# Transformer layer on eight cores: latent weights through the f32 queue, head 0's projections among the latent jobs, value jobs in other steps

## The chip, the cores and the metric

The kernel runs on all eight cores of one Trainium2 chip. The time is device microseconds (us) of the slowest core for one execution. Each core has a tensor engine (PE), a vector engine (DVE), a scalar engine (ACT), GpSimd (POOL) and SyncE (SP); the last two mainly issue DMAs here. A core keeps data in SBUF, and matmuls write to PSUM, which has eight banks of 128 x 512 f32.

## The reference

One pre-norm layer on x of 4 x 2048 x 2048. Attention with a compressed latent for keys and values (16 heads of 128, latent width 512), then a feed-forward part with fp8 weights:

```python
lat = rmsnorm(x @ wkv_a_w.T, norm_w)          # x is layer-normalised before
kv = lat @ wkv_b_w.T                          # keys and values of all heads
q = (x @ wq_w.T + wq_b)                       # the upper 64 of 128 per head rotated
attn = softmax(where(causal, q k^T * scale))  # k rotated in the same way
x = x + (attn @ v) @ out_w.T + out_b
y = layernorm(x)
x = x + (silu(y@gate * gs) * (y@up * us)) @ down * ds   # inner width 6144
```

## The kernel before

Two cores share a batch row. A core owns eight of the sixteen 128-row tiles of the sequence (their queries, outputs and feed-forward part) and computes the latent, keys and values of all sixteen for itself. Nothing passes between cores. Every engine runs a program written out by hand (`sync_prog`, `gpsimd_prog`, `vector_prog`, `scalar_prog`, `tensor_prog`), and they wait for each other on counting semaphores; an engine runs its own list strictly in order. So the place of a job in each of five lists sets the order.

The front. For each of 16 tiles of x (buffers X, four in turn, f32, 1 MB each, loaded by SP): DVE takes statistics (L478), ACT the square root (`sqrt_var`, L681), DVE normalises to bf16 (XH, four buffers, L488), PE transposes in two halves (`transposes`, L781; banks 6 and 7), ACT copies to XQT (tiles 0 to 7, the core's own) or XOT (8 to 15) (`transposed`, L693). Four tiles are a block (tb); for each block PE computes four latent jobs `lat(tb, dl)` of 16 matmuls with 512 columns (L800; block 0 in two halves of 256), one for each 128 of the latent's width, in banks 0 to 3. ACT makes of each its square (LSQ, L699) and a scaled copy (LATU, L702) in `lat_out`. `sumsq` (L811), `rms` on ACT (L707), `diagonal` on DVE (L498) and `broadcast` on PE (L819, bank 5) give the rms factor, and DVE multiplies it in (`latent`, L506) to LATT. The latent weights WKVA are four DMAs from POOL's queue that read f32 and write bf16. In ACT's list `sqrt_var(n + 1)` stands ahead of `lat_out` of tile n. A matmul with M2s and C2Q (L938) makes a small table for the rotation; DVE waits for it after it has normalised tile 5.

Jobs outside the latent have names: Q (h, half; 16 matmuls, L835, copied by DVE L515), K (h, quarter; 4 matmuls, L844, copied by ACT L714), V (group of four heads, tile; 4 matmuls, L854, copied by DVE L528), N, X, Y (a bound for the exponents from the squared norms; small matmuls L863, L866, L869, then a chain of small DVE operations that ends in NEGB, L551), O (head, half; four transposes of the head's output, L885, copied to OT by ACT L718), P (output projection, L879). `first_plan` lists those of head 0: Q(0,0) stands after block 0, Q(0,1) after the last latent job, and then come K 0 to 3, V 0 to 15 and N, X, Y.

Attention. A head has twelve steps. In step s PE runs the scores of the next step (L898), then the filling jobs of `head_plan(h)` for this step, then the values of the step before (L919). The filling jobs are those of the next head (Q, K, N, X, Y), four V jobs of the next group (heads 0 to 11), and O of this head's first half and the last head's second. ACT runs exp (L729) and the copies, DVE masks (L557), normalises the head's output (ON, L566 and L570) and copies. K, V and O share bank 7, so each waits until the one before it is copied (`ring_free`).

After attention come the output projection, the residual and second norm, and the feed-forward part; the change does not touch these.

Of the kernel before, what the change touches and what calls it, by code (L numbers as in the profile page):

```python
# [8 lines left out]
F32 = mybir.dt.float32  # L9
# [15 lines left out]
def head_plan(h):  # L25

    steps = [[] for _ in range(12)]
    ends = [[] for _ in range(12)]  # L30

    def put(s, job, lo=0, n=None):
        n = UNITS[job[0]] if n is None else n
        steps[s].append((job, lo, n))
        if lo + n == UNITS[job[0]]:
            ends[s].append(job)

    if h < 15:
# [24 lines left out]
    if h == 15:  # L63
        for s, d, lo, n in ([(s, 0, 2 * s, 2) for s in range(6)] + [(s, 1, 3 * s - 18, 3) for s in range(6, 10)]
                            + [(10, 0, 12, 4), (11, 1, 12, 4)]):
            put(s, ("P", 0, d), lo, n)
    return steps, ends


def first_plan():  # L70

    jobs = [("K", 0, 0), ("K", 0, 1), ("V", 0, 0), ("K", 0, 2), ("V", 0, 1), ("V", 0, 2), ("V", 0, 3), ("K", 0, 3),
            ("V", 0, 4), ("V", 0, 5), ("V", 0, 6), ("N", 0), ("V", 0, 7), ("V", 0, 8), ("X", 0), ("V", 0, 9),
            ("V", 0, 10), ("Y", 0)]
    jobs += [("V", 0, tt) for tt in range(11, 16)]
    return [(job, 6 + i % 2 if i < 8 else 4 + i % 4) for i, job in enumerate(jobs)]
# [20 lines left out]
def build_nc():  # L97
# [175 lines left out]
    s_k = sem("s_k")  # L273
    s_o = sem("s_o")
# [25 lines left out]
    order = []  # L300
    for n in range(16):
        order += [(("T", n, half), 6 + half) for half in range(2)]
        if n in (7, 15):
            order.append((("Q", 0, n // 8), 6))
# [14 lines left out]

    def ring(job):  # L320
        return BANK[job]

    def ring_prev(job):
        return BEFORE[job]

# [26 lines left out]
    def sync_prog(e):  # L352
        for n in range(4):
            e.dma_start(out=X[n][:, :], in_=xq_d.ap()[n * 128:(n + 1) * 128, :]).then_inc(d_x[n], 16)
            if n == 0:
                e.dma_start(out=CB[:, :], in_=cb_d.ap()[:, :]).then_inc(d_idb, 16)
                e.dma_start(out=CF[:, :], in_=cf_d.ap()[:, :]).then_inc(d_const, 16)
                e.dma_start(out=C2s[0:64, :], in_=c2_d.ap()[:, :]).then_inc(d_const, 16)
                e.dma_start(out=M2s[0:64, :], in_=m2_d.ap()[:, :]).then_inc(d_const, 16)
        for n in range(4, 16):  # L360
            src = xq_d if n < 8 else xo_d
            e.wait_ge(v_xh, n - 3)
            e.dma_start(out=X[n % 4][:, :], in_=src.ap()[(n % 8) * 128:(n % 8 + 1) * 128, :]).then_inc(d_x[n % 4], 16)
        e.wait_ge(v_latt, 16)
# [44 lines left out]
    def gpsimd_prog(e):  # L409
        for dl in range(4):  # L410
            e.wait_ge(d_x[dl // 2], 16)
            e.dma_start(out=WKVA[dl][:, :], in_=wkva_d.ap()[dl, :, :]).then_inc(d_wkva[dl], 16)

# [8 lines left out]
        for h in range(16):  # L422
            if h == 0:
                e.wait_ge(v_var, 3)
            elif h == 1:
                e.wait_ge(v_xh, 14)
            elif h >= 3:
                e.wait_ge(t_q, count(("Q", h - 3, 1)))
            e.dma_start(out=WQ[h % 3][:, :], in_=wq_d.ap()[h, :, :]).then_inc(d_wq[h % 3], 16)
            if h >= 2:  # L430
                e.wait_ge(t_k, count(("K", h - 2, 3)))
            e.dma_start(out=WK[h % 2][:, :], in_=wk_d.ap()[h, :, :]).then_inc(d_wk[h % 2], 16)
            if h in (0, 1, 3, 7):
# [33 lines left out]
    def vector_prog(e):  # L467
# [41 lines left out]
        def evict(job):  # L509
# [15 lines left out]
            elif kind == "V":  # L525
                _, g, tt = job
                e.wait_ge(t_v, count(job))
# [50 lines left out]
        for n in range(16):  # L578
# [11 lines left out]
            if n == 7:  # L590
                evict(("Q", 0, 0))
# [6 lines left out]
        e.wait_ge(t_lat, 16)  # L598
        for g in range(2):
            e.memset(A(VB[g], 128, [[8320, 128], [VW, 64]]), 1.0).then_inc(v_ones, 1)  # L600
        evict(("Q", 0, 1))
        diagonal(3)
        latent(3)
        for job, _ in first_plan():
            evict(job)
# [70 lines left out]
    def scalar_prog(e):  # L676
# [6 lines left out]
        def transposed(n):  # L683
            for half in range(2):
# [4 lines left out]
                elif n < 16:  # L689
                    out = A(XOT[n // 4 - 2], half * 8 * 512 + (n % 4) * 128, [[8192, 128], [512, 8], [1, 128]])  # L690
                else:
                    out = A(X2T, half * 8 * 1024 + (n - 16) * 128, [[16384, 128], [1024, 8], [1, 128]])
                e.activation(out, bankb(ring(job)), AFT.Identity).then_inc(s_t, 1)  # L693

        def lat_out(tb, dl):
# [36 lines left out]
        sqrt_var(0)  # L732
        for n in range(16):
            if n < 15:
                sqrt_var(n + 1)
            if n == 4:
                e.wait_ge(d_const, 48)
            if n >= 4:
                lat_out(n // 4 - 1, n % 4)
            transposed(n)  # L740
            if n in (8, 12):
                rms(n // 4 - 2)
        for dl in range(4):
            lat_out(3, dl)
            if dl == 0:
                rms(2)
        rms(3)
        for job, _ in first_plan():
            evict(job)
# [18 lines left out]
    def tensor_prog(e):  # L768
        def ring_free(job):
            before = ring_prev(job)  # L770
            if before is not None:
                e.wait_ge(EVICTED[before[0]], count(before))
# [12 lines left out]
        def xh_block(c, tb):  # L785
            if tb < 2:
                return XQT[:, c * 1024 + tb * 512:c * 1024 + tb * 512 + 512]
            return XOT[tb - 2][:, c * 512:(c + 1) * 512]

        def lat(tb, dl, lo=0, hi=512):  # L790
            if lo == 0:
                if tb == 0:
                    e.wait_ge(d_wkva[dl], 16)
                else:
                    e.wait_ge(s_lat, 4 * (tb - 1) + dl + 1)
            if dl == 0:
# [24 lines left out]
        def work(job, lo, n):  # L821
# [81 lines left out]
        def values(gs):  # L903
            h, s, qb, j, off = step(gs)
            g = h // 4
            if s == 0 and h % 4 == 0:
                e.wait_ge(v_v, count(("V", g, 15)))
# [19 lines left out]
        for n in range(2):  # L927
            transposes(n, XH[n])
        for dl in range(4):
            lat(0, dl, 0, 256)  # L930
            if dl % 2 == 1:
                transposes(2 + dl // 2, XH[2 + dl // 2])
        for dl in range(4):
            lat(0, dl, 256, 512)
            transposes(4 + dl, XH[dl])
            if dl == 0:
                e.wait_ge(v_c2, 1)
                e.matmul(bank(5, 0, 16), M2s[0:64, :], C2Q[0:64, 0:16], start=True, stop=True).then_inc(t_rope, 1)  # L938
        work(("Q", 0, 0), 0, 16)
        for tb in range(1, 3):  # L940
            for dl in range(4):
                lat(tb, dl)
                transposes(4 * (tb + 1) + dl, XH[dl])
# [4 lines left out]
        lat(3, 0)  # L948
        sumsq(2)
        lat(3, 1)  # L950
        broadcast(2)
        lat(3, 2)
        lat(3, 3)
        work(("Q", 0, 1), 0, 16)
        sumsq(3)
        for job, b in first_plan():
            work(job, 0, UNITS[job[0]])
            if job == ("K", 0, 2):
                broadcast(3)
# [145 lines left out]
```

## Time and profile before

| | us |
|---|---|
| median of 3 runs | 1682.87 (1682.58 to 1682.89) |
| the profiled execution | 1683.09 |
| its span on the slowest core | 1681.4 |
| PE busy | 1589.9 (95%) |
| DVE busy | 482.2 (29%) |
| ACT busy | 366.4 (22%) |
| POOL busy | 68.6 (4%) |

The profile is one execution on the slowest core; its own time is 0.2 us above the median. Busy time of PE includes the ends of pipelined matmuls, so a busy PE can still be waiting in part. L-numbers are lines of the kernel before. PE's clock has two levels; a granted clock of 1.00 in a stretch is the full 2.4 GHz throughout, and 0.5 would be 1.2 GHz throughout.

### The profile page before, as it was taken

What the parts mean: (1) busy time and instruction counts of PE and PEld (TensorE: products, weight loads), DVE (VectorE), ACT (ScalarE), POOL (GpSimd) and SP (SyncE); (2) the same over time, 40 slices, a digit from 0 to 9 for tenths busy, and PEclk for the clock granted to TensorE, in tenths of its full rate; (3) what the DMA queues carried; (4) which work ended last, traced back from release to release, by engine and by line L of the source; (5) the groups of instructions that cost most, each with busy time, mean ns of one, the idle gap of its engine ahead of it and who ended that gap; (6) DMA issues with size and microseconds to landing.
All of it is one profiled execution on the core that took longest, in us unless ns stands there. A gap on an engine that the chain in (4) does not pass through costs nothing.

```text
span 1681.4 us, 23380 instructions; the slowest of 8 cores (1677.7 to 1681.4 us)
## 1 busy us (share of the span) xinstructions
PE 1589.9 (95%) x9034; PEld 780.4 (46%) x9034; DVE 482.2 (29%) x1061; ACT 366.4 (22%) x496; POOL 68.6 (4%) x132
## 2 busy tenths in 40 slices
PE   3888998989999899999999999999999999999999
PEld 2543555555555444444444444444444444444444
DVE  5655444454444566211111111111111111111111
ACT  2542555555556311100000000110000000000000
POOL 1000001000000000000000000000000000000000
PEclk9999999999999999999999999999999999999999
DMA  9631325111132692435374547464434092939210
GB/s 243 196 88 42 57 54 87 29 29 21 28 45 52 121 230 101 94 32 47 29 63 39 50 39 63 40 55 38 46 34 42 0 97 66 92 84 103 75 53 32
DMA packets 33098, 115.04 MB, mean 68 GB/s; under 512 B 3744, under 2 KB 6112, under 8 KB 28640
## 3 DMA queue, kind: packets, MB, share of 16 engines
q0 software_dynamic: 18432, 60.83, 34.3%
q1 hardware_dynamic: 14560, 52.73, 9.5%
q8 instruction: 75, 1.23, 0.3%
q14 instruction: 31, 0.25, 0.1%
HBM read 233.08 MB, written 16.78 MB: 149 GB/s over the span
## 4 chain that ended last, share of the span: by engine, by line
PE 88%; DVE 4%; issue 3%; DMA 3%; ACT 2%; DVEq 0%; SPq 0%; ACTq 0%; POOL 0%; POOLq 0%
PE PS L1022 20%; PE PS L1002 20%; PE PS L1008 20%; PE PS L835 7%; PE PS L984 6%; PE PS L844 3%; PE PS L854 3%; PE PS L898 3%; PE PS L919 3%; PE PS L800 2%; DMA WKVA<-wkva 2%; DMA RES<-xq 1%; PE PS L781 1%; PE PS L879 1%; DMA X<-xq 0%
## 5 line engine op out<-in xcount | busy, mean ns | idle before, releaser
L1002 PE MATMUL PS<-X2T,W 128*128 128x512 bf16 x1536 | 347.2, 379 | 1.1 <-DVE RES L611 1.1
L1008 PE MATMUL PS<-X2T,W 128*128 128x512 bf16 x1536 | 347.2, 379 | 0.0
L663 DVE SCALAR_TENSOR_TENSOR FUSE<-PS,CF,SIL 128x512 bf16<-128x512 f32 x96 | 72.1, 751 | 589.8 <-PE PS L1008 581.3
L1002 PEld LDWEIGHTS PS<-X2T,W 128*128 128x128 fp8e4 x1536 | 150.2, 98 | 182.2 <-issue 1.5
L1008 PEld LDWEIGHTS PS<-X2T,W 128*128 128x128 fp8e4 x1536 | 150.3, 98 | 181.3
L729 ACT ACTIVATE P<-PS,NEGB 128x1024 bf16<-128x1024 f32 x192 | 172.7, 902 | 150.4 <-PE PS L898 145.2
L766 ACT ACTIVATE SIL<-PS,CF 128x512 bf16<-128x512 f32 x96 | 66.0, 688 | 584.6 <-PE PS L1002 584.6
L1022 PE MATMUL PS<-WDa,FUSE 128*128 128x512 fp8e4 x768 | 166.1, 379 | 1.2 <-DVE FUSE L663 1.2
L1022 PE MATMUL PS<-WDb,FUSE 128*128 128x512 fp8e4 x768 | 166.1, 379 | 0.0
L835 PE MATMUL PS<-XQT,WQ 128*128 128x512 bf16 x512 | 134.5, 383 | 1.3 <-ACT XQT L693 0.9
L1022 PEld LDWEIGHTS PS<-WDa,FUSE 128*128 128x128 bf16 x768 | 75.0, 98 | 92.1 <-issue 1.6
L1022 PEld LDWEIGHTS PS<-WDb,FUSE 128*128 128x128 bf16 x768 | 75.2, 98 | 90.6
L672 DVE TENSOR_TENSOR OB<-PS,DSC 128x512 f32<-128x512 f32 x32 | 22.1, 692 | 283.9 <-PE PS L1022 283.9
L984 PE MATMUL PS<-WO,OT 128*128 128x512 bf16 x448 | 98.0, 379 | 0.0
L854 PE MATMUL PS<-WV,LATT 128*128 128x512 bf16 x256 | 65.7, 386 | 33.3 <-ACT OT L718 20.4
L835 PEld LDWEIGHTS PS<-XQT,WQ 128*128 128x128 bf16 x512 | 49.2, 99 | 51.5 <-issue 4.4
L844 PE MATMUL PS<-LATT,WK 128*128 128x512 bf16 x256 | 65.6, 379 | 2.2 <-DVE QBa L515 0.9
L984 PEld LDWEIGHTS PS<-WO,OT 128*128 128x128 bf16 x448 | 43.5, 98 | 51.0
L919 PE MATMUL PS<-VBb,P 128*128 128x129 bf16 x576 | 48.5, 220 | 5.2 <-DVE P L557 3.4
L450 POOL DMA_DIRECT2D W<-gu x44 | 23.2, 528 | 691.8 <-PE PS L1008 691.8
L854 PEld LDWEIGHTS PS<-WV,LATT 128*128 128x128 bf16 x256 | 21.7, 98 | 63.5 <-issue 46.6
L919 PEld LDWEIGHTS PS<-VBb,P 128*128 128x128 bf16 x576 | 38.7, 98 | 24.1 <-issue 7.7
(121 smaller groups left out, 1072.1 us busy)
## 6 DMA issues: line engine op xcount, KB each, us to landing
W<-gu POOLq DMA_DIRECT2D x48, 512.0 KB, 8.8
X<-xq SPq DMA_DIRECT2D x8, 1024.0 KB, 13.4
WQ<-wq POOLq DMA_DIRECT2D x16, 512.0 KB, 5.5
X<-xo SPq DMA_DIRECT2D x8, 1024.0 KB, 5.4
WO<-wo POOLq DMA_DIRECT2D x16, 512.0 KB, 9.9
RES<-xq SPq DMA_DIRECT2D x8, 1024.0 KB, 14.8
res_scr<-RES SPq DMA_DIRECT2D x8, 1024.0 KB, 5.3
RB<-res_scr SPq DMA_DIRECT2D x32, 256.0 KB, 3.9
```

The source lines that it names most:

```text
L663: e.scalar_tensor_tensor(FUSE[:, io * 1024 + qb * 512:io * 1024 + qb * 512 + 512], bank(2 * (f % 3) + 1), USC[:, io:io + 1], SIL[f % 3][:, ...
L729: e.activation(p_ap(gs, off, w), A(PS, (gs % 2) * 1024 + off, [[4096, 128], [512, 2], [1, w]]), AFT.Exp, bias=NEGB[:, h % 2:h % 2 + 1], sc ...
L766: e.activation(SIL[f % 3][:, :], bank(2 * (f % 3)), AFT.Silu, scale=GSC[:, io:io + 1]).then_inc(s_silu, 1)
L835: mm = e.matmul(bank(b), WQ[h % 3][:, c * 128:(c + 1) * 128], xh_block(c, qb), start=(c == 0), stop=(c == 15))
L844: mm = e.matmul(bank(b), WK[h % 2][:, dl * 128:(dl + 1) * 128], LATT[:, dl * 2048 + tb * 512:dl * 2048 + tb * 512 + 512], start=(dl == 0), ...
L854: mm = e.matmul(bank(b), LATT[:, dl * 2048 + tt * 128:dl * 2048 + (tt + 1) * 128], WV[g % 2][:, dl * 512:(dl + 1) * 512], start=(dl == 0), ...
L898: mm = e.matmul(PS[:, (gs % 2) * 1024 + o * 512 + off:(gs % 2) * 1024 + o * 512 + 512], KB[h % 2][:, o * 1024 + j * 128:o * 1024 + (j + 1) ...
L919: mm = e.matmul(bank(4 + bk, 256 * (i % 2), 256 * (i % 2) + 129), P[gs % 4][:, o * 512 + i * 128:o * 512 + (i + 1) * 128], A(VB[g % 2], (( ...
L984: mm = e.matmul(bank(d), OT[:, c * 1024 + t * 128:c * 1024 + (t + 1) * 128], WO[c][:, d * 512:(d + 1) * 512], start=(c == 0), stop=(c == 15))
L1002: mm = e.matmul(bank(2 * (f % 3)), W8[io % 4][:, c * 128:(c + 1) * 128], X2T[:, c * 1024 + qb * 512:c * 1024 + qb * 512 + 512], start=(c = ...
L1008: mm = e.matmul(bank(2 * (f % 3) + 1), W8[io % 4][:, 2048 + c * 128:2048 + (c + 1) * 128], X2T[:, c * 1024 + qb * 512:c * 1024 + qb * 512 ...
L1022: mm = e.matmul(bank(6 + m % 2), FUSE[:, c * 1024 + t * 128:c * 1024 + (t + 1) * 128], WD[db % 2][:, c * 512:(c + 1) * 512], start=(c == 0 ...
```

## The change

1. The latent weights are loaded by SP as f32 into four staging buffers (WST), in one queue with the tiles of x and in a fixed order with them; ACT casts each to bf16 (`cast(dl)`, after the copies of tiles 0, 1, 3 and 4), and PE waits for the cast. POOL issues head 0's WQ, WK and WV after tile 4 is normalised, head 1's after the twelfth latent job.
2. `first_plan` is a new order, and twelve of its jobs stand between latent jobs (`SIDE`): Q(0,0), K 0, V 0, V 1 after block 1; V 2, V 3 and K 1, V 4, V 5 in and after block 2; V 6, V 7 and Q(0,1) in and after block 3. K 2, K 3, V 8 to 15, N, X, Y follow. Latent jobs of blocks 1 to 3 use banks 0 and 1 in turn, so banks 2 and 3 are free for these jobs. ACT copies V 0 to 7 of group 0 instead of DVE.
3. In ACT's list from tile 8 on, `lat_out` stands ahead of `tile(n)`, which holds `sqrt_var(n + 1)`. PE's order of transposes and half latent jobs in block 0 is new. DVE copies Q(0,0) after tile 11 instead of tile 7.
4. XOT is four buffers of half the size in other places.
5. In each head O(h,0) stands in step 5 instead of 6, and the V jobs in steps 6, 7, 9, 11 instead of 6, 8, 10, 11.

```diff
-            for i, st in enumerate((6, 8, 10, 11)):
+            for i, st in enumerate((6, 7, 9, 11)):
...
-        if s == 6:
+        if s == 5:
             put(s, ("O", h, 0))
...
+    q, k, v = (lambda i: ("Q", 0, i)), (lambda i: ("K", 0, i)), (lambda i: ("V", 0, i))
+    return [(q(0), 2), (k(0), 3), (v(0), 2), (v(1), 3), (v(2), 2), (v(3), 3), (k(1), 2), (v(4), 3), (v(5), 2),
+            (v(6), 3), (v(7), 2), (q(1), 3), (k(2), 6), (v(8), 7), (v(9), 2), (v(10), 6), (v(11), 7), (k(3), 2),
+            (v(12), 4), (v(13), 6), (("N", 0), 7), (v(14), 4), (("X", 0), 6), (v(15), 5), (("Y", 0), 7)]
...
+    SIDE[1, 3] = PLANNED[0:4]
+    SIDE[2, 0] = PLANNED[4:5]
+    SIDE[2, 1] = PLANNED[5:6]
+    SIDE[2, 3] = PLANNED[6:9]
+    SIDE[3, 0] = PLANNED[9:10]
+    SIDE[3, 1] = PLANNED[10:11]
+    SIDE[3, 3] = PLANNED[11:12]
...
+        load_x(1)
+        load_wkva(0)
+        load_x(2)
+        load_wkva(1)
+        load_x(3)
+        load_x(4)
+        load_wkva(2)
+        load_x(5)
+        load_wkva(3)
+        for n in range(6, 16):
+            load_x(n)
...
-        for dl in range(4):
-            e.wait_ge(d_x[dl // 2], 16)
-            e.dma_start(out=WKVA[dl][:, :], in_=wkva_d.ap()[dl, :, :]).then_inc(d_wkva[dl], 16)
...
-            if n == 7:
+            if n == 11:
                 evict(("Q", 0, 0))
...
+        def cast(dl):
+            e.wait_ge(d_wkva[dl], 16)
+            e.activation(WKVA[dl][:, :], WST[dl][:, :], AFT.Identity).then_inc(s_cast, 1)
...
+        def tile(n):
             if n < 15:
                 sqrt_var(n + 1)
+            if n == 8:
+                e.wait_ge(s_cast, 4)
             transposed(n)
+
+        sqrt_var(0)
+        for n in range(6):
+            tile(n)
+            if n in (0, 1, 3, 4):
+                cast((0, 1, 3, 4).index(n))
+        e.wait_ge(d_const, 48)
+        lat_out(0, 0)
+        tile(6)
+        for dl in range(1, 4):
+            lat_out(0, dl)
+        tile(7)
+        for tb in range(1, 4):
+            for dl in range(4):
+                lat_out(tb, dl)
+                if tb < 3:
+                    tile(4 * tb + 4 + dl)
+                if dl == 0:
+                    rms(tb - 1)
+                for job in SIDE[tb, dl]:
+                    evict(job)
...
+        transposes(0, XH[0])
+        transposes(1, XH[1])
+        lat(0, 0, 0, 256)
+        lat(0, 1, 0, 256)
+        transposes(2, XH[2])
+        transposes(3, XH[3])
+        lat(0, 2, 0, 256)
+        transposes(4, XH[0])
+        lat(0, 3, 0, 256)
+        lat(0, 0, 256, 512)
+        e.wait_ge(v_c2, 1)
+        e.matmul(bank(5, 0, 16), M2s[0:64, :], C2Q[0:64, 0:16], start=True, stop=True).then_inc(t_rope, 1)
+        transposes(5, XH[1])
+        lat(0, 1, 256, 512)
+        transposes(6, XH[2])
+        lat(0, 2, 256, 512)
+        lat(0, 3, 256, 512)
+        transposes(7, XH[3])
+        for tb in range(1, 4):
             for dl in range(4):
                 lat(tb, dl)
-                transposes(4 * (tb + 1) + dl, XH[dl])
+                if tb < 3:
+                    transposes(4 * (tb + 1) + dl, XH[dl])
                 if dl == 0:
                     sumsq(tb - 1)
                 if dl == 1:
                     broadcast(tb - 1)
+                run(SIDE[tb, dl])
+        sumsq(3)
+        run(PLANNED[12:15])
+        broadcast(3)
+        run(PLANNED[15:])
```

## Rows read from the trace of the kernel before

**Rows 1.** The page: the chain that ended last, its shares by engine.
```profile
PE 88%; DVE 4%; issue 3%; DMA 3%; ACT 2%; DVEq 0%; SPq 0%; ACTq 0%; POOL 0%; POOLq 0%
```
**Rows 2.** Stretches: window, length, busy us of each engine, PE clock, DMA share, GB/s.
```profile
17.00:61.00 44.00, 28.91 (x258) 23.80 (x258) 29.51 (x53) 20.38 (x31) 2.17 (x3) 0.92 0.98 257
132.50:162.65 30.15, 25.55 (x144) 11.25 (x143) 17.32 (x40) 3.83 (x7) 1.07 (x2) 0.94 0.22 57
214.70:241.30 26.60, 24.15 (x198) 13.66 (x196) 13.03 (x39) 14.07 (x18) 2.12 (x4) 1.00 0.38 66
```
**Rows 3.** DMA queues from 0 to 190 us: packets, MB written, share of 16 engines.
```profile
q1 hardware_dynamic: 2896, 18.13, 28.8%
q0 software_dynamic: 2304, 6.82, 21.3%
```
**Rows 4.** Timeline to 61 us: start, us, engine, line, operation, count [idle before, releaser].
```profile
8.10 2.47 DVE L478 BATCH_NORM_STATS2 BNSa<-X 128x6 f32<-128x512 f32 x4 [6.71 <-DMA X<-xq]
...
15.60 1.35 DVE L488 TENSOR_SCALAR XH<-X,MV,RSTD 128x2048 bf16<-128x2048 f32 x1
...
39.76 3.57 PE L800 MATMUL PS<-XQT,WKVA 128*128 128x256 bf16 x16 [4.73 <-DMA WKVA<-wkva]
...
44.28 1.94 ACT L693 ACTIVATE XQT<-PS 128x1024 bf16<-128x1024 bf16 x2 [9.70 <-PE PS L781]
...
50.23 2.47 DVE L478 BATCH_NORM_STATS2 BNSb<-X 128x6 f32<-128x512 f32 x4 [0.17 <-DVE WQBG L589]
...
59.25 1.05 PE L781 MATMUL PS<-CB,XH 128*128 128x128 bf16 x16 [1.54 <-DVE XH L488]
```
**Rows 5.** Timeline from 61 to 133 us, blocks 1 to 3.
```profile
61.23 5.30 PE L835 MATMUL PS<-XQT,WQ 128*128 128x512 bf16 x16 [0.92 <-ACT XQT L693]
...
74.10 0.68 ACT L702 ACTIVATE LATUb<-PS,CF 128x512 f32<-128x512 f32 x1
...
82.28 2.47 DVE L506 TENSOR_TENSOR LATT<-LATUa,PS 128x512 bf16<-128x512 f32 x4
...
115.73 5.30 PE L800 MATMUL PS<-XOTb,WKVA 128*128 128x512 bf16 x16 [2.41 <-ACT XOTb L693]
...
125.58 7.07 PE L800 MATMUL PS<-XOTb,WKVA 128*128 128x512 bf16 x32
```
**Rows 6.** Timeline from 145 to 166 us, the end of the front.
```profile
145.72 4.33 PE L854 MATMUL PS<-WV,LATT 128*128 128x512 bf16 x12 [3.51 <-DVE VBa L528]
...
163.38 1.28 ACT L729 ACT_TABLE_LOAD   x1 [11.66 <-PE PS L898]
...
164.67 1.91 ACT L729 ACTIVATE P<-PS,NEGB 128x1024 bf16<-128x1024 f32 x2
...
165.93 0.38 PE L898 MATMUL PS<-QBa,KBa 128*128 128x256 bf16 x2
```
**Rows 7.** Timeline of head 2, steps 4 to 6.
```profile
229.14 0.28 PE L919 MATMUL PS<-VBa,P 128*128 128x129 bf16 x2
...
229.81 0.61 DVE L570 TENSOR_SCALAR ONa<-PS,RL 128x128 bf16<-128x128 f32 x2
...
233.93 1.02 PE L854 MATMUL PS<-WV,LATT 128*128 128x512 bf16 x4 [1.68 <-ACT OT L718]
```
**Rows 8.** Timeline of head 1, steps 9 to 11.
```profile
212.50 0.38 PE L869 MATMUL PS<-DG,ONEF 2*128 2x2 f32 x2
...
214.75 0.15 DVE L551 TENSOR_SCALAR NEGB<-YT 128x1 f32<-128x1 f32 x1 [0.17 <-DVE YT L548]
...
215.06 0.68 DVE L528 CAST VBb<-PS 128x512 bf16<-128x512 f32 x1
...
215.89 1.02 PE L854 MATMUL PS<-WV,LATT 128*128 128x512 bf16 x4 [0.71 <-DVE VBb L528]
```
**Rows 9.** Waits of PE from 188 to 500 us: us in total, times, longest.
```profile
PE PS L854 <- ACT OT L718: 18.6, 11, 1.8
```
**Rows 10.** Timeline of head 12, step 9: Y where no V job stands ahead.
```profile
502.92 0.35 PE L869 MATMUL PS<-DG,ONEF 2*128 2x2 f32 x2 [0.31 <-DVE DG L537]
```

More of the change, by code:

```diff
@@ L299, in build_nc @@
     PLAN = [head_plan(h) for h in range(16)]
[L300 to L304, printed above, removed]
+    order = [(("T", n, half), 6 + half) for n in range(16) for half in range(2)]
     order += first_plan()
@@ L318, in build_nc, with evicted @@
         latest[b] = job
+    def evicted(job):
+        if job[0] == "V":
+            return (s_v, job[2] + 1) if job[1] == 0 and job[2] < 8 else (v_v, count(job) - 8)
+        return EVICTED[job[0]], count(job)
     def ring(job):
@@ L324, in ring_prev, with lat_bank @@
         return BEFORE[job]
+    PLANNED = [job for job, _ in first_plan()]
+    SIDE = {(tb, dl): [] for tb in range(1, 4) for dl in range(4)}
+    SIDE[1, 3] = PLANNED[0:4]
[5 more added lines that the diff above has]
+    SIDE[3, 3] = PLANNED[11:12]
+    def lat_bank(tb, dl):
+        return dl if tb == 0 else dl % 2
     def step(gs):
@@ L352, in sync_prog, with load_x, load_wkva @@
     def sync_prog(e):
[L353 to L360, printed above, removed]
+        def load_x(n):
+            if n >= 4:
+                e.wait_ge(v_xh, n - 3)
             src = xq_d if n < 8 else xo_d
-            e.wait_ge(v_xh, n - 3)
             e.dma_start(out=X[n % 4][:, :], in_=src.ap()[(n % 8) * 128:(n % 8 + 1) * 128, :]).then_inc(d_x[n % 4], 16)
+        def load_wkva(dl):
+            e.dma_start(out=WST[dl][:, :], in_=wkva_d.ap()[dl, :, :]).then_inc(d_wkva[dl], 16)
+        load_x(0)
+        e.dma_start(out=CB[:, :], in_=cb_d.ap()[:, :]).then_inc(d_idb, 16)
+        e.dma_start(out=CF[:, :], in_=cf_d.ap()[:, :]).then_inc(d_const, 16)
+        e.dma_start(out=C2s[0:64, :], in_=c2_d.ap()[:, :]).then_inc(d_const, 16)
+        e.dma_start(out=M2s[0:64, :], in_=m2_d.ap()[:, :]).then_inc(d_const, 16)
+        load_x(1)
[9 more added lines that the diff above has]
+            load_x(n)
         e.wait_ge(v_latt, 16)
@@ L526, in evict @@
                 _, g, tt = job
+                if g == 0 and tt < 8:
+                    return
                 e.wait_ge(t_v, count(job))
@@ L597, in vector_prog @@
         latent(2)
-        e.wait_ge(t_lat, 16)
-        for g in range(2):
-            e.memset(A(VB[g], 128, [[8320, 128], [VW, 64]]), 1.0).then_inc(v_ones, 1)
         evict(("Q", 0, 1))
         diagonal(3)
-        latent(3)
+        for g in range(2):
+            e.wait_ge(t_lat, 16)
+            e.memset(A(VB[g], 128, [[8320, 128], [VW, 64]]), 1.0).then_inc(v_ones, 1)
         for job, _ in first_plan():
-            evict(job)
+            if job[0] != "Q":
+                evict(job)
+            if job == ("V", 0, 9):
+                latent(3)
         def add(t, d):
@@ L689, in transposed @@
                 elif n < 16:
-                    out = A(XOT[n // 4 - 2], half * 8 * 512 + (n % 4) * 128, [[8192, 128], [512, 8], [1, 128]])
+                    out = A(XOT[n // 4 - 2][half], (n % 4) * 128, [[4096, 128], [512, 8], [1, 128]])
                 else:
@@ L714, in evict @@
                 e.activation(KB[h % 2][:, tb * 512:(tb + 1) * 512], bank(ring(job)), AFT.Identity).then_inc(s_k, 1)
+            elif job[0] == "V" and job[1] == 0 and job[2] < 8:
+                _, g, tt = job
+                e.wait_ge(t_v, count(job))
+                e.activation(A(VB[0], tt * 4 * VW, [[8320, 128], [VW, 4], [1, 128]]), bank(ring(job)),
+                             AFT.Identity).then_inc(s_v, 1)
             elif job[0] == "O":
@@ L771, in ring_free @@
             if before is not None:
[L772 removed]
+                e.wait_ge(*evicted(before))
         def transposes(n, xh):
@@ L926, in tensor_prog, with run @@
         e.wait_ge(d_idb, 16)
[L927 to L940, printed above, removed]
+        def run(jobs):
+            for job in jobs:
+                if job == ("Q", 0, 0):
+                    e.wait_ge(s_lat, 4)
+                work(job, 0, UNITS[job[0]])
+        transposes(0, XH[0])
[17 more added lines that the diff above has]
+        for tb in range(1, 4):
             for dl in range(4):
                 lat(tb, dl)
-                transposes(4 * (tb + 1) + dl, XH[dl])
+                if tb < 3:
+                    transposes(4 * (tb + 1) + dl, XH[dl])
                 if dl == 0:
```

59 lines of the change are left out of this document (19 added, 40 removed).

## The prediction

> **What bounds the kernel now.** I read the chain of waits first: 88% of it is TensorE (PE) work [rows 1], so the kernel is a PE kernel, and a change can win only where PE stands still. The stretches show where that is [rows 2]. From 17 to 61 us PE is busy for 28.9 of 44 us while the DMA engines are 98% busy; from 132.5 to 162.65 us, the last stretch before attention, 25.6 of 30.2; in a whole head (214.7 to 241.3 us) 24.15 of 26.6. The feed-forward part is not touched. So the change acts in two places: the front (0 to 165.9 us, where the third scores of head 0 start [rows 6]) and twelve heads of 26.6 us, with four shorter ones. I lay both out again, instruction by instruction in each engine's new order, with durations of the rows.
>
> **Part 1, latent weights through SP in f32, cast on ACT.** The queues show no saving of DMA time: in the first 190 us q1 spends 28.8% of 16 engines on 18.13 MB, which is 48 engine-us per MB, and q0 21.3% on 6.82 MB, 95 per MB written [rows 3]. q0 reads twice what it writes, so both pay 48 per MB read; 1.05 MB take 3.2 us. What changes is the order. Now x tiles and weights share the engines and the last weights land at 39.7 us, so PE waits 4.73 us for them [rows 4]; afterwards everything comes in one line. With the first statistics still at 8.1 us I get landings of x1 12.0, w0 15.2, x2 18.3, w1 21.5, x3 24.6, x4 27.8, w2 30.9, x5 34.1, w3 37.3, x6 40.4 us. One tile costs DVE 2.47 (statistics) and 1.35 (normalise), with the small operations 4.35 [rows 4].
>
> The 48 engine-us per MB are 331 GB/s, with both queues at work for most of it [rows 3]. The Trainium skill, page "DMA: Bandwidth & Descriptors", section Specifications, gives about 358 GB/s as what HBM leaves to one core; by it, as an estimate, a tile takes 2.9 us, x4 lands 1.4 us sooner, and the sum below would be 17.9 instead of 16.5. The rows decide for me.
>
> The cast isn't in the trace. The nearest rows are ACT's copies: two of 1024 columns take 1.94 us together [rows 4]. So one of 2048 costs 1.0 (if SBUF to SBUF went at twice the pace) to 2.5 us; I take 1.9. Four of them are 7.6 us of ACT, which is idle for half of this stretch, but two lie on the path, because cast 2 stands behind tile 3's copies and cast 3 behind tile 4's. Worked on: tile 3 is normalised at 33.1, its copies end at 36.7, cast 2 at 38.6, the latent job at 42.3 (3.57 us, the slow form after idling [rows 4]), tile 4 transposed 43.9, copied 45.4, cast 3 47.3. Then two latent half jobs (1.9 each, or 3.6 if the clock is still at 1.2 GHz) and the rope matmul, for which DVE waits after tile 5. The statistics of tile 7 start at 52.3 to 54.0 us, where they start at 50.23 now [rows 4]: the front is 2 to 4 us LATER here. Two tiles of DVE on, tile 7 is ready at 61 to 63 us instead of 59.
>
> **Part 2, head 0's projections between latent jobs.** Nothing is added in work; ten jobs of four matmuls (K 0, K 1, V 0 to 7; 0.86 us each at PE's pace) leave the stretch behind the last latent job, and Q(0,0) leaves its place ahead of block 1. Now Q(0,0) delays that block (5.30 us at the low clock [rows 5]) while the copies of tile 7 end. Afterwards latent job (1,0) starts at about 65.4 to 67, with the slow form (5.3) since PE has idled; from there PE has the pace 3.5 (latent job, 7.07 for two) [rows 5] plus 1.06 (transposes [rows 4]) and DVE 4.35 a tile, plus 2.47 for each latent product [rows 5] and about 1 for each diagonal's small operations. I get tile 11 normalised at 88.2 and transposed at 89.4. Then Q(0,0), K 0, V 0, V 1 run in the hole in which PE now waits for ACT's copies. DVE waits there for Q(0,0), up to 92.9, which puts tile 12 at 98.0; PE reaches it at 99.0, so this costs nothing yet. Block 2 ends with tile 15 at 116.6 and has carried V 2 and V 3; K 1, V 4, V 5 then stand in the hole of 2.41 us ahead of latent job (3,0), which was also at the low clock, 5.30 [rows 5]. It now starts at 119.2 at full clock. The last latent job ends at 136.2, Q(0,1) at 139.6. Now both are over at 135.9 (latent jobs 115.73 to 132.6 [rows 5], then 3.5 of Q): PE is 3.7 us later, but with ten jobs done, 8.6 us. Net gain here 4.9.
>
> Edits with one answer: the split of the transposed tiles over four buffers and two instead of four latent banks cost nothing, since each latent job waits for a copy that ended a job ago (0.5 + 0.68 us of ACT [rows 5] within 3.5 us of PE). Eight V copies (0.68 [rows 8]) moved to ACT relieve DVE by 5.5 us. WQ, WK, WV of head 0 are issued after tile 4 (38 us), needed at 89; those of head 1 at 116, needed at 154: covered, as a load behind one queue needs under 10 us.
>
> The tail: behind Q(0,1) come K 2, V 8, V 9 (142.7), the broadcast (143.8; DVE's copy of Q and the diagonal are ready at 142.7), V 10, V 11 (145.5), then K 3 must wait for the last latent product, 147.0: a stall of 1.5 in place of 3.51 [rows 6]. N waits 0.6 more for the squares of K, X and Y follow, Y at 153.35. Scores(0) can start at 153.7. But exp(0) waits for Y's chain on DVE, 2.4 us after Y (as from 212.50 to 214.90 [rows 8]), and then for the table load of 1.28 us [rows 6]: exp at 157.1, ended at 158.1, scores(2) at 158.3 us. Now that point is 165.93 [rows 6]. Front: 7.6 us gained, 1.9 of Y's chain exposed in it.
>
> At the table load the rows show exp starting 0.01 us behind it (163.38 + 1.28, then 164.67) [rows 6]. The Trainium skill, page "ScalarE: Activation LUTs", section "What ACT_TABLE_LOAD costs", adds a drain of 1.38 us to it; by that the front would gain 6.2, as an estimate. The rows decide for me.
>
> **Part 3, the heads.** O(h,0) goes from step 6 to 5, and the V jobs from 6, 8, 10, 11 to 6, 7, 9, 11. Removed: V in step 6 waits for ACT to empty the bank of O, 1.68 us [rows 7], eleven times for 18.6 us [rows 9] and once in head 0. Added: O(h,0) now stands right behind scores(6), and its input is ready only 1.28 us after values(3) start (229.14, to the end of ONa at 230.42) plus 0.15; PE is there 0.55 after them. A stall of 0.88 in each of 16 heads. O's copy ends 1.2 us ahead of V in step 6: no wait is left there. Next, step 8 has no V job between X and Y, and Y waits for DVE 0.2 to 0.3, as in the heads without V jobs [rows 10]. Step 11: V waits for the copy of the V before it, 0.71 now [rows 8]. Its predecessor is a step earlier, but its copy stands behind Y's chain on DVE (2.4 us): I get 0.62 instead of 0.87 from end to start, and K at the next head's step 0 waits 0.4 rather than 0.2. Laid out from values(3) of one head to scores(1) of the next: 13.40 us for 14.44, less 0.17 for K: 0.87 a head, 10.4 in twelve. Heads 12 to 14 only pay: 0.8 each, 2.4. Head 15 has a projection job in step 6 that needs O's bank too, and wins 0.9. Sum 8.9.
>
> **Total.** 7.6 + 8.9 = 16.5 us. The profiled execution took 1683.1 (span 1681.4 and 1.7 around it), 0.2 over the median; so 1666.6 by its own time, 1666.5 against the median.
>
> **The rivals.**
> Front without gain: cast or clock cost more (casts 2.5 us, both half jobs and Q(0,0) at the low clock: 1.2 + 3.4 + 1.8), or tiles 12 to 15, which now hang on DVE's wait for Q(0,0), fall behind PE by a tile's statistics, 2.5 us. For it: PE's clock level is 0.92 from 17 to 61 us [rows 2]. Against: later stages have slack. 1683.1 - 8.9 = 1674.
> More than forecast: casts half as dear and DMA quicker than in the rows (4), V at step 11 without a wait (0.6 in twelve heads, 7, half of it likely): 1657 to 1660.
> Heads without gain: O's wait of 0.88 and the waits on DVE eat the 1.7: 1683.1 - 7.6 = 1675.5. If both fail, the change does not do what it says: 1683.
> Slower: ACT now takes the square root for tile n+1 only behind the copies of the latent job (before, ahead of them). Then tile n+1 can be normalised only after latent job, copies (1.2), root (0.3), normalise (1.6). While that, 3.1 us, is under the next latent job's 3.5, it is hidden. It decides once ACT is later by over 0.4 us, say by a tile's copies of 1.94: then 3.1 stand openly in each of up to eight tiles, 25 us, and 1666.6 + 25 = 1691.6. Against: ACT has under half of its time busy in these stages, and the copies fit behind the transposes.
>
> **How the numbers follow.** Forecast 0.45 (own range 1661 to 1672, from the cast's bounds, the clock and 0.4 us a head), front without gain 0.15, more than forecast 0.17, heads without gain 0.10, both 0.06, slower 0.07. The range from 1656 to 1679 leaves out both failing, slower, and a little on the low side. 0.2% is 3.4 us, about what a measurement of this kernel can tell from no change. Faster 0.86, same 0.06, slower 0.08.
>
> **What would show it.** In the new trace: statistics of tile 7 at 52 to 54 us; latent job (3,0) at full clock near 119; scores(2) of head 0 near 158.3; no wait of V on OT, but O(h,0) waiting 0.9 us for ON in step 5; head period 25.7 us in heads 1 to 11, and 0.8 more in 12 to 14. The prediction is wrong if a tile's transposes wait for DVE behind ACT's roots from tile 9 on, or if the period stays at 26.6.

## The result and the profile after

| | before | after |
|---|---|---|
| median, us | 1682.88 | 1670.78 |
| ratio to before | | 0.9924 (0.9907 to 0.9942) |
| profiled execution, us | 1683.1 | 1671.0 |
| span of the slowest core, us | 1681.4 (core 7) | 1669.5 (core 2) |
| mean span of the eight cores, us | 1679.0 | 1666.8 |

The change makes the kernel 12.1 us faster; 16.4 were forecast (1666.5), with a range of 1656 to 1679 and 0.86 on faster. Below, a time of an experiment is its ratio to before times 1682.9, because before itself read 1682.8 us in the session of e1 to e4, 1684.4 in that of e5 to e8 and 1683.2 in that of e9 to e12. The ratios leave out executions in which the cores of one die ran slower.

The page of the changed kernel: busy time by engine, and the shares of the chain that ended last.

```profile
PE 1581.0 (95%) x8897; PEld 779.7 (47%) x9034; DVE 477.4 (29%) x1053; ACT 377.7 (23%) x508; POOL 65.9 (4%) x128
...
PE 89%; DVE 4%; DMA 3%; issue 2%; ACT 1%; SPq 0%; DVEq 0%; ACTq 0%
```

The stretches of the changed kernel, columns as in [rows 2]: the first block, and one whole head (from scores(2) of a head to those of the next).

```profile
17.00:61.00 44.00, 25.99 (x195) 19.94 (x196) 26.65 (x48) 21.08 (x24) 1.74 (x3) 0.88 0.89 274
...
215.89:241.59 25.70, 23.93 (x197) 13.57 (x197) 13.03 (x39) 14.09 (x19) 2.12 (x4) 1.00 0.40 68
```

Against [rows 2]: the head is 0.90 us shorter (26.60 to 25.70). From 17 to 61 us PE and DVE have done less than before, the DMA engines are busy for less of the time (0.89 for 0.98), and PE's granted clock is lower (0.88 for 0.92). That GB/s is higher (274 for 257) says nothing of the pace: the rate counts what is written, and the latent weights are now written as f32, twice the bytes.

Three points in each core's trace split the time. Statistics of tile 7 mark the end of DVE's wait for the rotation matmul (the small matmul with M2s and C2Q), scores(2) of head 0 the end of the front, the first transposes behind attention the end of the heads. Means of the eight cores in the one profiled execution of each kernel, us:

| | tile 7's statistics | scores(2) | end of the heads | span |
|---|---|---|---|---|
| before | 49.4 | 163.8 | 580.6 | 1679.0 |
| after | 54.4 | 161.9 | 568.4 | 1666.8 |
| change | +5.0 | -1.9 | -12.2 | -12.2 |

So the heads give 10.3 us, the front 1.9, and what follows the heads nothing. The front starts by losing 5.0.

### The profile page after: what moved, and what is told of

The parts are those of the page before. It is cut to its first block, busy times and chain, and to the rows that moved or that the text cites. A ratio compares the mean times of both kernels' runs of the same rounds, so it can differ in the third digit from the quotient of the medians.

```text
span 1669.5 us, 23252 instructions; the slowest of 8 cores (1663.9 to 1669.5 us)
## 1 busy us (share of the span) xinstructions
PE 1581.0 (95%) x8897; PEld 779.7 (47%) x9034; DVE 477.4 (29%) x1053; ACT 377.7 (23%) x508; POOL 65.9 (4%) x128
## 4 chain that ended last, share of the span: by engine, by line
PE 89%; DVE 4%; DMA 3%; issue 2%; ACT 1%; SPq 0%; DVEq 0%; ACTq 0%
PE PS L1083 20%; PE PS L1063 20%; PE PS L1069 20%; PE PS L890 7%; PE PS L1045 6%; PE PS L975 3%; PE PS L899 3%; PE PS L909 3%; PE PS L854 3%; PE PS L953 3%; DMA X<-xq 2%; PE PS L835 1%; DMA RES<-xq 1%; PE PS L934 1%; DVE ONa L600 1%
## 5 line engine op out<-in xcount | busy, mean ns | idle before, releaser
L705 DVE TENSOR_TENSOR OB<-PS,DSC 128x512 f32<-128x512 f32 x32 | 22.1, 692 | 283.9 <-PE PS L1083 283.9
L909 PE MATMUL PS<-WV,LATT 128*128 128x512 bf16 x235 | 60.8, 379 | 11.1 <-DVE P L587 4.3
L975 PEld LDWEIGHTS PS<-VBa,P 128*128 128x128 bf16 x576 | 39.5, 98 | 20.7 <-issue 1.8
## 6 DMA issues: line engine op xcount, KB each, us to landing
X<-xq SPq DMA_DIRECT2D x8, 1024.0 KB, 10.3
```

What stands on the lines that cost most here:

```text
L909: mm = e.matmul(bank(b), LATT[:, dl * 2048 + tt * 128:dl * 2048 + (tt + 1) * 128], WV[g % 2][:, dl * 512:(dl + 1) * 512], start=(dl == 0), ...
L975: mm = e.matmul(bank(4 + bk, 256 * (i % 2), 256 * (i % 2) + 129), P[gs % 4][:, o * 512 + i * 128:o * 512 + (i + 1) * 128], A(VB[g % 2], (( ...
```

## The experiments

Three questions. Do the heads' edits alone give the heads' gain, and which of the two? Are the casts, or what they do to PE's clock and to DVE's wait, the loss in the first block (theory A, with its parts A1 place and C clock)? Or is the front bound elsewhere: by the landings of x, by PE's pace, by ACT's roots (rivals)?

| kernel | ratio to before | us |
|---|---|---|
| e1, before + both edits of the heads | 0.9943 (0.9930 to 0.9956) | 1673.3 |
| e2, before + O in step 5 only | 0.9939 (0.9926 to 0.9952) | 1672.6 |
| e8, before + V steps only | 1.0005 (0.9995 to 1.0014) | 1683.7 |
| the changed kernel | 0.9924 (0.9907 to 0.9942) | 1670.1 |
| e3, changed, weights cast by POOL's DMAs | 0.9894 (0.9880 to 0.9909) | 1665.1 |
| e4, changed, rotation copied after tile 8 | 0.9901 (0.9884 to 0.9919) | 1666.2 |
| e5, e3 and e4 together | 0.9871 (0.9854 to 0.9889) | 1661.2 |
| e7, changed, idle matmuls in three waits | 0.9894 (0.9879 to 0.9908) | 1665.1 |
| e6, changed, casts 2 and 3 one place sooner | 0.9870 (0.9855 to 0.9884) | 1661.0 |
| e9, e6 and e4 together | 0.9867 (0.9852 to 0.9881) | 1660.5 |
| e10, e6, idle matmuls before job (1,0) | 0.9872 (0.9855 to 0.9888) | 1661.4 |
| e11, e6, ACT's root first again | 0.9868 (0.9852 to 0.9885) | 1660.7 |
| e12, e9, V steps of before | 0.9866 (0.9846 to 0.9886) | 1660.3 |

**The heads: e1, e2, e8.** The edits, alone or together, on the kernel before:

```diff
-            for i, st in enumerate((6, 8, 10, 11)):
+            for i, st in enumerate((6, 7, 9, 11)):      # e1, e8
...
-        if s == 6:
+        if s == 5:                                      # e1, e2
             put(s, ("O", h, 0))
```

> The kernel before with only the two edits of the heads: O of the first half in step 5, V jobs in steps 6, 7, 9, 11. The front is that of before. If the hand layout of the heads holds (theory A: the wait on O's copy gone, a smaller wait on ON in its place), it is 9 to 11 us faster than before: the changed kernel's gain of 12.1 us less the 1.9 us that its front gained on the mean of the eight cores. If the heads' gain needs the new front, or the whole gain is the front's (rival), within 3 us of before.

> The kernel before with only O of the first half in step 5 and the V jobs where they were (6, 8, 10, 11). Theory A (O's move carries the gain, the V jobs' new steps pay for it): the wait of V on O's copy (1.7 in twelve heads, 20 us) goes, 0.75 a head for ON comes (12 us), V in step 11 waits for V in step 10 as before, Y doesn't wait (0.2 to 0.3 in twelve heads): 7 to 12 us faster than before, and not slower than the kernel with both edits by more than 3 us. Rival (the V steps carry it, O's move only exchanges waits): within 3 us of before.

> The kernel before with only the V jobs in steps 6, 7, 9, 11; O of the first half stays in step 6. With the O edit alone at 1672.6 and both at 1673.3, the V edit should be worth nothing or cost up to 1 us by itself: theory A (the wait on O's copy stays, Y waits 0.2 to 0.3 more in twelve heads, the copy in step 9 stands behind Y's chain): 1682 to 1686, no faster than before. Rival (either edit alone removes the shared loss around bank 7, so they don't add): 1675 to 1680.

Measured: 9.6, 10.3 and no gain (the interval reaches from 0.8 faster to 2.4 slower). In the traces attention, from scores(2) of head 0 to the end of the heads, takes 407.3, 406.8 and 417.6 us on the mean of cores, 416.8 before. The waits of PE from 188 to 500 us (columns as in [rows 9]); first e1:

```profile
PE PS L885 <- DVE ONa L570: 8.8, 12, 1.1
PE PS L854 <- DVE VBb L528: 4.3, 8, 0.9
PE PS L854 <- DVE VBa L528: 2.4, 4, 0.9
PE PS L869 <- DVE DG L537: 1.7, 9, 0.2
```

and e8:

```profile
PE PS L854 <- ACT OT L718: 18.6, 11, 1.8
PE PS L854 <- DVE VBb L528: 4.3, 8, 0.9
PE PS L854 <- DVE VBa L528: 2.4, 4, 0.9
PE PS L869 <- DVE DG L537: 2.1, 10, 0.3
```

e8 keeps the wait on O's copy in full, 18.6 us as in [rows 9]; e1 hasn't got it and waits 8.8 us for ON instead. That exchange is the gain. The V steps only make the waits on VB smaller and add those on DG. Theory A holds for both; the rival that the V steps carry something falls.

**Part 1 undone: e3.**

```diff
-        load_wkva(0)                       # and 1 to 3, in SP's list
...
+        for dl in range(4):                # in POOL's list, bf16 by the DMA
+            e.wait_ge(d_x[dl // 2], 16)
+            e.dma_start(out=WKVA[dl][:, :], in_=wkva_d.ap()[dl, :, :]).then_inc(d_wkva[dl], 16)
...
-            if n in (0, 1, 3, 4):
-                cast((0, 1, 3, 4).index(n))
...
-                    e.wait_ge(s_cast, dl + 1)
+                    e.wait_ge(d_wkva[dl], 16)
```

> The changed kernel with its part 1 undone: the latent weights come through POOL's queue and are cast by the DMA, as before; ACT casts nothing and SP loads x alone; all the rest as changed. Theory A (the casts behind tile copies and the slow clock they leave PE with hold back the rotation matmul, for which DVE waits: statistics of tile 7 at 54.4 us on the mean of cores against 49.4 before): tile 7's statistics start at 47 to 50 us and the time falls by 4 to 6 us against the changed kernel, to about 1665 to 1667. Rival (the first block doesn't matter, the later tiles' chain through ACT's roots or PE's pace sets the front): the same as the changed kernel, 1670 to 1672. Second rival (the DMA queue order helps): slower than the changed kernel by 2 or more.

Measured: 5.0 us less than the changed kernel, tile 7's statistics at 48.7 us on the mean of cores (54.4 with the change), scores(2) at 155.6 (161.9). Theory A's numbers. Both rivals fall: whatever the queue order of part 1 brings is less than what the casts cost in this place, and the first block does set the front. One piece of part 1 stays in e3: POOL still issues head 0's WQ, WK and WV only after tile 4.

**DVE's wait moved: e4, and both: e5.**

```diff
-            if n == 5:
+            if n == 8:
                 e.wait_ge(t_rope, 1)
```

> The changed kernel, but DVE waits for the rotation matmul and copies its result after tile 8 instead of after tile 5. Theory A (DVE stands 10.0 us there with tiles 6 and 7 landed): statistics of tile 7 start at 45 to 48 us, tile 7 is transposed 2 to 5 us sooner, since PE still has late half jobs, and the time falls by 3 to 5 us to 1666 to 1668. Rival (PE's casts and half jobs are the limit and DVE's wait is only a symptom): within 1.5 us of the changed kernel's 1670.8.

> Both of the last two edits on the changed kernel: weights cast by POOL's DMAs, and DVE waits for the rotation matmul after tile 8. If the two losses are separate and add up (5.5 and 4.5 us), 1661. Theory A says they are one loss seen twice (the casts delay the matmul for which DVE waits), with a rest: in the kernel with POOL's weights DVE still stands about 3 us before tile 7's statistics; so 1 to 3 us below the 1665.3 of POOL's weights alone, 1662.5 to 1664.5. If the x tiles' landings hold the first block by now (rival), 1665 as with POOL's weights alone.

Measured: e4 gains 3.9 us on the changed kernel, e5 another 3.9 on e3. e4 went as theory A said. For e5 I had expected 1 to 3 us below e3, and by the ratios it is beyond that, though the two intervals overlap. The traces narrow it: scores(2) is at 154.6 us on the mean of cores in e5 and at 155.6 in e3, 1.0 sooner. The session of e5 was itself later there: e8, whose front is that of before, has scores(2) at 165.5, while before has 163.8 and e1 and e2, with the same front, 163.9 and 164.0. So e4's edit is worth 1.0 to 2.7 us on top of e3, less than the 3.8 that it moves scores(2) of the changed kernel (161.9 to 158.1): the two losses overlap in part, as expected. What DVE stood still for in the changed kernel is plain in its waits from 40 to 66 us:

```profile
DVE WROPE L618 <- PE PS L1000: 10.0, 1, 10.0
DVE BNSa L506 <- DMA X<-xq: 1.6, 1, 1.6
```

10.0 us for the rotation matmul, for which it stood 1.3 before.

**Place and clock: e6, e7.** e6 keeps all four casts and their length, and moves two of them by one tile:

```diff
-            if n in (0, 1, 3, 4):
-                cast((0, 1, 3, 4).index(n))
+            if n < 4:
+                cast(n)
```

> The changed kernel with casts 2 and 3 one place sooner in ACT's list: behind the copies of tiles 2 and 3 instead of 3 and 4. Theory A1 (the place behind a tile's copies costs, not the 1.9 us of the cast): latent half jobs (0,2) and (0,3) start without waits of 3.2 and 3.5 us, tile 7's statistics move from 54.4 to 50 to 52 us on the mean of cores, and the time falls by 2 to 4.5 us to 1666.5 to 1669. Rival A2 (f32 weights land too late in the one queue, so a cast that is asked for sooner makes ACT wait for the DMA and holds the tile's copies): 1670 or slower.

e7 leaves the casts and gives PE something to do in the waits:

```diff
+        warm(9)      # nine matmuls of 512 columns into bank 4, read by nobody
         lat(0, 2, 0, 256)
         transposes(4, XH[0])
+        warm(9)
...
         transposes(7, XH[3])
+        warm(9)
```

> The changed kernel with 27 idle matmuls of 512 columns into the unused bank 4: nine each before the latent half job (0,2), behind the transposes of tile 4 (before half job (0,3)) and before latent job (1,0), where PE waits about 3 us each time. They add work but no data. Theory C (the low clock after these waits is a part of the loss: half jobs take 3.2 to 3.6 us instead of 1.9, and job (1,0) 5.1 instead of 3.5): those jobs run at full clock, the rotation matmul comes 2 to 3 us sooner, and 2 to 5 us are gained in all: 1666 to 1669. Rival (the clock costs nothing, since other waits take up what it gives back; the idle matmuls themselves take 1.9 to 3.8 us each time): 1671 to 1674.

Measured: e6 9.1 us, far more than the 2 to 4.5 expected, and by 4.1 us more than taking the casts away (e3; the two intervals overlap at their ends, and the traces have 1.2 at scores(2), with e6 in the later session); e7 5.0 us with 27 matmuls more than the changed kernel has. On the mean of cores scores(2) moves from 161.9 to 154.4 in e6 and to 159.1 in e7, 7.5 and 2.8 us, in that later session. The timeline of the changed kernel, from the copies of tiles 2 and 3 on, with casts 2 and 3 (counted from 0; columns as in [rows 4]):

```profile
35.18 1.94 ACT L726 ACTIVATE XQT<-PS 128x1024 bf16<-128x1024 bf16 x2 [5.14 <-PE PS L835]
...
37.19 1.94 ACT L726 ACTIVATE XQT<-PS 128x1024 bf16<-128x1024 bf16 x2
...
39.00 1.93 ACT L740 ACTIVATE WKVA<-WST 128x2048 bf16<-128x2048 f32 x1
...
41.07 3.40 PE L854 MATMUL PS<-XQT,WKVA 128*128 128x256 bf16 x16 [3.20 <-ACT WKVA L740]
...
44.31 1.06 PE L835 MATMUL PS<-CB,XH 128*128 128x128 bf16 x16
45.01 1.94 ACT L726 ACTIVATE XQT<-PS 128x1024 bf16<-128x1024 bf16 x2 [3.91 <-PE PS L835]
46.84 1.91 ACT L740 ACTIVATE WKVA<-WST 128x2048 bf16<-128x2048 f32 x1
...
48.89 6.33 PE L854 MATMUL PS<-XQT,WKVA 128*128 128x256 bf16 x32 [3.53 <-ACT WKVA L740]
55.15 0.39 PE L1000 MATMUL PS<-C2Q,M2s 64*128 64x16 f32 x2
...
56.28 2.47 DVE L506 BATCH_NORM_STATS2 BNSb<-X 128x6 f32<-128x512 f32 x4 [0.17 <-DVE WQBG L619]
```

Each cast makes ACT's turn 1.9 us longer just where PE waits for it; PE waits 3.20 and 3.53 us, and the half jobs behind the waits go mostly at the low clock, 3.40 and 6.33 for two where 1.91 and 3.65 are the full pace. PE's granted clock is 0.54 from 41.10 to 44.40 us and 0.56 from 48.95 to 55.10. The same stretch in e6:

```profile
38.53 1.91 PE L854 MATMUL PS<-XQT,WKVA 128*128 128x256 bf16 x16 [1.19 <-ACT WKVA L740]
...
40.88 1.05 PE L835 MATMUL PS<-CB,XH 128*128 128x128 bf16 x16 [0.45 <-DVE XH L516]
...
42.34 3.65 PE L854 MATMUL PS<-XQT,WKVA 128*128 128x256 bf16 x32 [0.40 <-ACT WKVA L740]
...
45.92 0.39 PE L1000 MATMUL PS<-C2Q,M2s 64*128 64x16 f32 x2
```

The waits are 1.19 and 0.40, the jobs run at a granted clock of 1.00, and the rotation matmul is at 45.92 instead of 55.15 (each in its slowest core; on the mean of cores tile 7's statistics move from 54.4 to 47.0, where 50 to 52 were expected). And in e7:

```profile
41.72 1.91 PE L854 MATMUL PS<-XQT,WKVA 128*128 128x256 bf16 x16 [1.26 <-ACT WKVA L740]
...
48.05 3.65 PE L854 MATMUL PS<-XQT,WKVA 128*128 128x256 bf16 x32 [1.59 <-ACT WKVA L740]
51.64 0.39 PE L1006 MATMUL PS<-C2Q,M2s 64*128 64x16 f32 x2
```

The casts are where they were in the list, and the half jobs start at 41.72 and 48.05 us, close to the 41.07 and 48.89 of the changed kernel, but they run at a granted clock of 1.00: 3.5 us of the 9.2 us by which e6 brings the rotation matmul forward. So A1 and C both hold, and they are not independent: the waits bring the low clock. The rival A2 (weights land too late for a sooner cast) falls.

**Behind the first block: e9, e10, e11, e12.** All on e6: e9 has e4's edit; e10 the nine idle matmuls behind tile 7's transposes only; e11 `sqrt_var(n + 1)` ahead of `lat_out(tb, dl)` again; e12 is e9 with the V steps of before.

> The kernel with the casts one place sooner (e6_cast_early, 0.987 of before), and DVE's wait for the rotation matmul moved behind tile 8. If DVE's stand is by now a symptom that the sooner casts removed (theory A: it had 10.0 us there in the changed kernel, about 0.5 in this one), nothing: 0.986 to 0.988 of before. If the two losses add (rival): 0.984 to 0.985.

> e6_cast_early with nine idle matmuls of 512 columns behind the transposes of tile 7, where PE waits 2.75 us for ACT's copies before latent job (1,0), which takes 5.1 us at the low clock instead of 3.5. Theory C (the clock is a loss of its own in this place): job (1,0) at full clock, 1.0 to 1.7 us less, 0.986 of before. Rival: PE is ahead of DVE from tile 9 on and the gain is taken up there, or the idle matmuls (1.9 to 3.8 us) run past the wait: 0.987 to 0.989.

> e6_cast_early with ACT's square root for tile n+1 ahead of the copies of the latent job again from tile 8 on, as in the kernel before. The prediction's slower rival lived on the new order (DVE waits up to 4.6 us for ACT's root at tile 9 and under 1.5 at others, but PE waits for DVE only at tile 11, 2.3 us). Theory A (that order is hidden, PE paces this stretch): within 0.1% of e6_cast_early, 0.986 to 0.988 of before. Rival (the order costs a part of what the front lost, DVE could run ahead and tile 11 would be ready sooner): 1.5 to 3 us faster, 0.985 to 0.986.

> e9_cast_rope with the V jobs back in steps 6, 8, 10, 11 (O of the first half stays in step 5). The V edit alone was worth nothing (1.0005 of before) and O alone 10.2 us against 9.5 for both. Theory A: the V steps are worth 0 to 1 us the wrong way here too, so 0 to 1 us faster than e9_cast_rope. Rival: with the wait on O's copy gone the V steps matter (in the changed kernel attention took 0.4 us less than with O alone): 0.3 to 1 us slower than e9_cast_rope.

All four are within 0.7 us of e6, less than their intervals (2.4 to 3.4 us to either side) tell apart. e9: no gain from DVE's wait can be told once the casts are sooner (theory A). e12: the V steps are worth nothing that can be told here either, so neither its theory nor its rival is shown. e10: in its trace job (1,0) does run at full clock,

```profile
56.88 2.10 PE L1008 MATMUL PS<-CB 128*128 128x512 bf16 x9
59.58 3.61 PE L854 MATMUL PS<-XQT,WKVA 128*128 128x512 bf16 x16 [0.59 <-ACT XQT L726]
```

where e6 has 5.08 us for it, and yet no gain can be told (its rival). Two cores of e6's own trace show the same without an edit: core 5 starts job (1,0) at 61.87 us and takes 5.30 for it, core 6 at 61.90 and takes 3.61, and their scores(2) start at 155.5 and 155.6. In all ten kernels with the new order of jobs (the changed kernel, e3 to e7, e9 to e12), job (1,0) starts at 58.0 to 68.4 us on the mean of cores, and scores(2) follows 93.2 to 94.8 us later, at whichever clock the job runs. So the clock was a loss ahead of the rotation matmul and none here, and what the experiments win in the front they win ahead of job (1,0). e11: with the root behind the copies DVE waits for it, in the changed kernel from 66 to 125 us

```profile
DVE RSTD L513 <- ACT SDb L714: 7.8, 3, 5.6
```

and in e11 that row is gone. The time is the same, and so is PE's one wait for DVE at a tile's transposes in this stretch (tile 11): 2.34 us in the changed kernel, 2.36 in e6, 2.35 in e11. So the wait for the root was hidden.

## Why the prediction was right or wrong

**The heads, right, and nearly in size.** "Sum 8.9": the heads' edits alone give 9.6, the heads' stretch of the changed kernel 10.3. The head period, forecast as 25.7, is 25.70. "A stall of 0.88 in each of 16 heads" is 0.71: in head 2 of the changed kernel

```profile
226.11 0.61 DVE L600 TENSOR_SCALAR ONa<-PS,RL 128x128 bf16<-128x128 f32 x2
226.87 0.38 PE L940 MATMUL PS<-CB,ONa 128*128 128x128 bf16 x4 [0.71 <-DVE ONa L600]
```

"Y waits for DVE 0.2 to 0.3": 2.1 us in eleven. The wait of V in step 11, 0.71 before, is 0.51:

```profile
237.89 1.02 PE L909 MATMUL PS<-WV,LATT 128*128 128x512 bf16 x4 [0.51 <-DVE VBb L558]
```

Heads 12 to 14 were to pay 0.8 each: from exp(0) of one head to that of the next they take 23.9, 22.8 and 22.7 us instead of 23.1, 21.7 and 21.7, so 0.8, 1.1 and 1.0. The rival "heads without gain" is out. That the V steps bring nothing was in the working (a wait smaller by 0.25 us a head in step 11 against 0.2 to 0.3 for Y; K's 0.17 makes it worse), though I hadn't said it as a result.

**Part 1, right in direction, too small.** A cast of 2048 columns, "I take 1.9" (from 1.0 to 2.5): 1.91. Of the four casts "two lie on the path": they do (e6). "The statistics of tile 7 start at 52.3 to 54.0": 56.28 in the profiled core, 54.4 on the mean. Of the 3.1 us by which the core misses the middle of that range, about 1.5 are landings: x1 was there at 13.7, not 12.0, tile 3 normalised at 34.9, not 33.1, and cast 3 ended at 48.8, not 47.3. The rest is the term "two latent half jobs (1.9 each, or 3.6 if the clock is still at 1.2 GHz)": I counted one slow job at most, and both were slow, 6.33 for 3.8 to 5.5. This is the step that was mis-sized: the low clock, priced as a surcharge on one job, lay on both half jobs ahead of the rotation matmul. And the price of the casts reaches on: without them (e3) scores(2) comes 6.3 us sooner on the mean of cores.

The rate of the queue. The first 190 us of the changed kernel in 40 slices of 4.75 us (GB/s):

```profile
GB/s 136 232 320 317 347 343 341 341 343 274 215 196 2 243 202 221 0 224 174 76 193 3 0 0 3 0 148 157 60 0 0 0 205 150 9 0 42 116 94 0
```

The fifth to the ninth slice (19 to 43 us) have the f32 queue nearly alone, and it reads at 341 to 347 where I took 331. The 358 of the Trainium skill (page "DMA: Bandwidth & Descriptors", section Specifications) is on the other side, and about as far off. No tile came sooner by it, because x1 came late: DVE started on tiles 2, 3, 5 and 6 at 20.4, 26.3, 35.2 and 41.2 us, as they landed, and the forecast landings were 18.3, 24.6, 34.1 and 40.4.

**Part 2, right from job (1,0) on, but started too late.** Latent job (1,0) "starts at about 65.4 to 67": 70.8 in the profiled core, 68.4 on the mean. Job (3,0) runs at full clock, as said, but at 125.4 instead of 119.2. From job (1,0) to the end of the last latent job I had 70.0 us and the trace has 71.3; from there to scores(2) I had 22.1 and it has 22.1 (142.15 to 164.24). Y's chain was exposed as said, and exp stands right behind the table load:

```profile
161.69 1.28 ACT L771 ACT_TABLE_LOAD   x1 [7.13 <-DVE NEGB L581]
...
162.98 1.90 ACT L771 ACTIVATE P<-PS,NEGB 128x1024 bf16<-128x1024 f32 x2
...
164.24 0.38 PE L953 MATMUL PS<-QBa,KBa 128*128 128x256 bf16 x2 [0.55 <-ACT P L771]
```

That is 0.01 us, as in [rows 6]; the drain of 1.38 us that the Trainium skill adds (page "ScalarE: Activation LUTs", section "What ACT_TABLE_LOAD costs") isn't seen here either, behind the load or ahead of it: NEGB ends at 161.60, the load starts at 161.69. So of the forecast 7.6 us for the front 1.7 came in the slowest core: 5.9 missing, of which 3.1 were lost ahead of tile 7, 1.5 between it and job (1,0) (the next half jobs were slow as well, 4.75 for two), and 1.3 in the blocks. The heads gave back 1.5. Of the rivals, "front without gain" described the mechanism best (casts or clock cost more), and the result lies between it and the forecast. That the total was near owes something to luck: of the front's 7.6 us less than a quarter came, and the heads' surplus made up a part.

**A reading that was too narrow.** The 165.93 us from which I counted the front's gain is that of the slowest of eight cores; the eight have 162.7 to 165.9 before and 159.2 to 164.2 after. A gain of a few us in a front that waits for DMA is of the size of that spread.

**The slower rival**, tiles waiting behind ACT's roots, is out: the transposes of tile 11 wait 2.3 us for DVE, but as long in e11, with the root first, and e11 shows that the order costs nothing that can be told. The new order of the front is worth 8.2 us on the mean of cores once its casts are gone (scores(2) 163.8 to 155.6 in e3), about what I forecast for the whole; the casts where they stood took 6.3 of it back.

## What to carry to other kernels

Two jobs of 1.9 us on an engine that had time to spare cost 9.1 us here, more than twice their own length, because they stood in its list just ahead of what another engine waited for: look at the place of such a job, and move it by one step before giving it up. When a stall at a start brings the tensor engine to its low clock, the matmuls behind each wait pay again (3.40 us for 1.91 here), and they may stand ahead of something that a third engine waits for; so price a wait in a front at both clock levels for all the jobs up to the next handover, not for the first alone. And follow who waits for a bank back to the copy that empties it: moving one small job of each head a step earlier (O) gave 10 us in all, moving the jobs that waited (V) gave nothing.

## What the runs showed of the hardware

- Nine matmuls of 512 columns whose result nobody reads, put into each of two waits of 3.20 and 3.53 us, brought the half jobs behind them from a granted clock of 0.54 and 0.56 to 1.00 (3.40 to 1.91 us, 6.33 for two to 3.65), though each nine take 2.1 us of PE. With nine more ahead of job (1,0) the whole kernel came 5.0 us forward (e7). In that third place alone, on e6, they brought the job to full clock (5.08 to 3.61) and the kernel nowhere (e10).
- f32 weights by SP with a cast on ACT and bf16 weights cast by POOL's DMAs can't be told apart when the casts stand in the right place and DVE's wait is moved in both: 0.9867 (e9) and 0.9871 (e5) of before.
- The fastest kernels here, e5, e6 and e9 to e12 at 0.987 of before, are 9 to 10 us faster than the changed kernel and 22 us faster than before. The smallest edit among them is two casts moved by one tile.
